# First attention: the values products put between the maxima and the scores of the next step, the maxima turned a step later, and all of the input biased ahead of the routing

## The reference

```python
x = layernorm(x + attention0(x))   # 16 heads of 8, causal, score - (i - j)
x = layernorm(x + mixture(x))      # 8 experts, each token goes to one: argmax(x @ centroids.T)
x = layernorm(x + attention1(x))   # 16 heads of 64, a gated distance bias, causal
x = layernorm(x + ffn(x))          # gated, 512 wide
# attention0 ends in  out @ Wo.T + bo ; the mixture starts with a layer norm of each token
```

## Time and profile before

| | us |
|---|---|
| median of 3 runs | 2271.55 (2269.65 to 2274.39) |
| the profiled execution, its own time | 2270.39 |
| its span in the trace | 2268.6 |
| first attention | up to 554.1 |
| routing: barrier to the last scatter issued | 554.5 to 624.2 |
| PE busy, whole span | 91% |

### The profile page before, as it was taken

The page is one execution under the profiler, slowest core; times in us unless marked ns, Lnnn a source line. Parts: engine busy times, 40 slices in busy tenths (PEclk is TensorE's granted clock), DMA queues, the critical chain, the costliest instruction groups (busy, mean ns, idle before and its releaser), DMA issues.

```text
span 2268.6 us, 34364 instructions
## 1 busy us (share of the span) xinstructions
PE 2053.4 (91%) x11728; PEld 1167.7 (51%) x11728; DVE 1373.6 (61%) x3345; ACT 1157.6 (51%) x1859; POOL 843.4 (37%) x544
## 2 busy tenths in 40 slices
PE   5799999998487879886899999999999999999998
PEld 2333333334476445444566556655666556655644
DVE  4777777774732678875566666666667655333311
ACT  2366666667343667674455555555555543223232
POOL 5000000000601445432577777777777773000000
PEclk8899999999589899996899999999999999999999
DMA  5233333111365579977667766776677677543300
GB/s 178 96 128 129 127 114 127 57 51 59 103 184 146 171 221 323 282 221 203 148 160 178 180 162 157 179 180 164 154 180 179 167 208 186 136 98 84 89 5 10
DMA packets 263468, 335.88 MB, mean 148 GB/s; under 512 B 22828, under 2 KB 185948, under 8 KB 262888
## 3 DMA queue, kind: packets, MB, share of 16 engines
q1 hardware_dynamic: 247992, 305.82, 50.2%
q0 software_dynamic: 7664, 24.39, 3.0%
q10 hardware_dynamic: 7640, 3.48, 0.5%
HBM read 193.69 MB, written 122.62 MB: 139 GB/s over the span
## 4 chain that ended last, share of the span: by engine, by line
PE 42%; issue 6%; DVE 4%; DMA 1%; SPq 0%; ACT 0%; DVEq 0%; ACTq 0%
PE ps L1284 10%; PE ps L953 7%; PE ps L937 6%; PE ps L906 6%; PE ps L938 6%; PE ps L1235 3%; DVE a1mx L1009 2%; PE ps L940 1%; PE ps L1295 1%; PE ps L1272 1%; PE ps L1273 1%; DVE a1mx L1005 1%; DMA a1FQ<-s_q 1%; DVE a1mx L1002 0%; PE ps L909 0%
## 5 line engine op out<-in xcount | busy, mean ns | idle before, releaser
L1120 POOL TENSOR_TENSOR a1sum<-a1sum,a1prob 128x1024 f32<-128x1024 f32 (+3 forms) x256 | 463.8, 1812 | 84.0 <-ACT a1prob L1063 51.2
L1063 ACT ACTIVATE a1prob<-ps 128x512 f32<-128x512 f32 (+2 forms) x640 | 328.0, 553 | 245.8 <-PE ps L940 214.5
L476 DVE TENSOR_REDUCE a0grid<-ps 128x8 f32<-128x1024 f32 x288 | 346.9, 1221 | 116.5 <-PE ps L351 71.9
L1002 DVE CUSTOM_DVE_ANT_0 ps<-ps,c_mask_ij 128x128 f32<-128x128 f32 x496 | 264.4, 551 | 194.3 <-issue 190.0
L577 ACT ACTIVATE a0prob<-ps 128x1024 f32<-128x1024 f32 x288 | 292.6, 1025 | 171.6 <-PE ps L377 91.5
L937 PE MATMUL ps<-a1QA,a1KA 69*128 69x512 f32 (+3 forms) x768 | 285.6, 379 | 5.0 <-DMA a1QA<-a1neg 5.0
L953 PE MATMUL ps<-a1prob,a1V 128*64 128x512 f32 (+3 forms) x1536 | 273.8, 499 | 5.0 <-ACT a1prob L1063 5.0
L938 PE MATMUL ps<-a1QB,a1KB 128*128 128x512 f32 (+3 forms) x768 | 264.3, 352 | 0.0
L906 PE MATMUL ps<-a1KA,a1QA 68*128 68x128 f32 x744 | 225.0, 381 | 4.6 <-DMA a1KA<-s_g 3.8
L953 PEld LDWEIGHTS ps<-a1prob,a1V 128*64 128x64 f32 x1536 | 102.9, 138 | 173.3 <-issue 138.7
L1005 DVE TENSOR_REDUCE a1mx<-ps 128x1 f32<-128x320 f32 x248 | 146.0, 589 | 70.5 <-PE ps L906 67.6
(11 more groups left out here) (267 smaller groups left out, 3196.1 us busy)
## 6 DMA issues: line engine op xcount, KB each, us to landing
a1FQ<-s_q SPq DMA_DIRECT2D x128, 256.0 KB, 7.9
a1KB<-s_k SPq DMA_DIRECT2D x128, 256.0 KB, 8.5
s_xs<-c_zero POOLq DMA_DIRECT2D x19, 1024.0 KB, 8.9
s_q<-mqkT SPq DMA_DIRECT2D x32, 512.0 KB, 3.4
s_v<-mv SPq DMA_DIRECT2D x32, 512.0 KB, 5.8
s_k<-a1KH SPq DMA_DIRECT2D x32, 512.0 KB, 5.0
s_k<-a1KL SPq DMA_DIRECT2D x32, 512.0 KB, 6.0
a1KA<-s_k SPq DMA_DIRECT2D x64, 256.0 KB
```

The source lines that it names most:

```text
L476: dve.tensor_reduce(grid[g % 2][:, :, a:b + 1:b - a], banks(("max", k)), axis=AX.X, op=ALU.max).then_inc(s1_free, 1)
L1002: dve.tensor_tensor_reduce(bank[:, 0:w], bank[:, 0:w], const["mask_ij"][:, BANK - w:BANK], 1.0, LOWEST, ALU.add, ALU.max, mx[:, x % 2, h, ...
L1063: act.activation(weights_of(g, u)[:, group[0]:group[-1] + 1, off:BANK], both(e, u, group), ACT.Exp).then_inc(weighed, 1)
L1120: pool.tensor_tensor(t[:, :, off:BANK], t[:, :, off:BANK], weights_of(g, u)[:, :, off:BANK], ALU.add).then_inc(summed, 1)
```

## The change

In the loop of PE, the values of the step before are issued between the maxima and the scores of a step, and the maxima are turned when k % NU is 2 instead of 1. In the routing, `x1` moves to memory that the first attention leaves free. SP loads the whole input into it ahead of the barrier, in two transfers of 1 MB, after the five small weights, and POOL biases all 8 chunks there ahead of the barrier, in place. `join` reads its chunk from `x1`, and `norm` writes it back there. Between the scatters POOL has nothing else to do, and SP has no loads to wait for.

```diff
-                if k % NU == 1 and NU < k <= TOTAL + 1:
+                if k % NU == 2 and NU < k <= TOTAL + 2:
                     turn_maxima(k // NU - 1)
+                if k > LEAD:
+                    g, u = divmod(k - 1 - LEAD, NU)
+                    if u in after:
+                        ...  # values(g - 1, r) and values(g, r), as below
                 if k < LEAD:
                     continue
                 g, u = divmod(k - LEAD, NU)
                 if g < GROUPS:
                     scores(k - LEAD)
-                if u in after:
-                    for r in after[u][0] if g > 0 else ():
-                        values(g - 1, r)
-                    for r in after[u][1] if g < GROUPS else ():
-                        values(g, r)
...
         def sync_ahead():
+            for d, s in first:
+                nc.sync.dma_start(d, s).then_inc(w_first, 16)
             load(0)
-            load(1)
-            for d, s in first: ...
+            load(1)          # load(half): 16 of the 32 tiles of x into x1
         def sync_first():
             ...
-            load(2)
             for d, s in rest:
                 nc.sync.dma_start(d, s).then_inc(w_rest, 16)
-            for c in range(3, steps):
-                load(c)
...
-                dve.tensor_tensor(r1[c % 2][:, :, :], tiles(ps[:, c % 2, :]), x[c % 2][:, :, :], ALU.add)
+                dve.tensor_tensor(r1[c % 2][:, :, :], tiles(ps[:, c % 2, :]), x1[:, c * TILES:(c + 1) * TILES, :], ALU.add)
...
         def gpsimd_ahead():
+            pool.wait_ge(w_first, 16 * len(first))
+            for c in range(steps):
+                pool.wait_ge(x_in[c // (steps // 2)], 16)
+                to = x1[:, c * TILES:(c + 1) * TILES, :]
+                pool.tensor_tensor(to, to, bo[:, :].unsqueeze(1).to_broadcast([P, TILES, P]), ALU.add).then_inc(biased, 1)
         def gpsimd_first():
             # only the 4 scatters of each chunk, no bias between them
```

More of the change, by code:

```diff
@@ L439, in tensor_program @@
                     drained(NPROD - 1)
-                if k % NU == 1 and NU < k <= TOTAL + 1:
+                if k % NU == 2 and NU < k <= TOTAL + 2:
                     turn_maxima(k // NU - 1)
+                if k > LEAD:
+                    g, u = divmod(k - 1 - LEAD, NU)
+                    if u in after:
+                        for r in after[u][0] if g > 0 else ():
+                            values(g - 1, r)
+                        for r in after[u][1] if g < GROUPS else ():
+                            values(g, r)
                 if k < LEAD:
@@ L1475, in middle @@
         jpos = own("jpos", [P, steps, TILES])
-        x1 = own("x1", [P, NTILE, P])
         stats, mv = own("st", [P, TILES, 6]), own("mv", [P, TILES, 2])
@@ L1504, in middle @@
         own("gap", [P, max(0, const["a0_end"] - nc.sbuf_base) // 4 + 8])
-        tri_f, x = own("trif", [P, P]), [own(f"xin{r}", [P, TILES, P]) for r in range(2)]
+        tri_f, x1 = own("trif", [P, P]), own("x1", [P, NTILE, P])
         wo, bo, cent = own("wo", [P, P]), own("bo", [P, P]), own("cent", [P, experts])
@@ L1529, in middle, with load @@
         PER = 6
[L1533 to L1537, removed]
+        def load(half):
+            t = slice(half * NTILE // 2, (half + 1) * NTILE // 2)
+            nc.sync.dma_start(x1[:, t, :], ins["x"][t.start * P:t.stop * P, :].rearrange("(t p) d -> p t d", p=P)).then_inc(x_in[half], 16)
         def sync_ahead():
+            for d, s in first:
+                nc.sync.dma_start(d, s).then_inc(w_first, 16)
             load(0)
             load(1)
-            for d, s in first:
-                nc.sync.dma_start(d, s).then_inc(w_first, 16)
         def sync_first():
@@ L1654, in join @@
                     dve.wait_ge(x1_full, c - 1)
-                dve.tensor_tensor(r1[c % 2][:, :, :], tiles(ps[:, c % 2, :]), x[c % 2][:, :, :], ALU.add).then_inc(joined, 1)
+                dve.tensor_tensor(r1[c % 2][:, :, :], tiles(ps[:, c % 2, :]), x1[:, c * TILES:(c + 1) * TILES, :], ALU.add).then_inc(joined, 1)
                 dve.wait_ge(joined, c + 1)
@@ L1824, in scalar_first, with gpsimd_ahead @@
             act.activation(om1[:, :], om1[:, :], ACT.Ln, bias=1.0).then_inc(rooted_u, 1)
-        def bias(c):
+        def gpsimd_ahead():
             pool = nc.gpsimd
[L1830 to L1837, removed]
+            pool.wait_ge(w_first, 16 * len(first))
[3 more added lines that the diff above has]
+                pool.tensor_tensor(to, to, bo[:, :].unsqueeze(1).to_broadcast([P, TILES, P]), ALU.add).then_inc(biased, 1)
         def gpsimd_first():
@@ L1842, in gpsimd_first @@
             pool.wait_ge(const["zeroed"], 16 * const["n_zeroed"])
[L1843 to L1852, removed]
+            for c in range(steps):
+                pool.wait_ge(dest_full, c + 1)
+                pool.wait_ge(xn_full, (c + 1) * TILES)
+                for t in range(TILES):
+                    pool.indirect_dma_start(scr["xs"][:, :], bass.IndirectOffsetOnAxis(dest[:, c * TILES + t:c * TILES + t + 1], 0),
+                                            xn[c % NS][:, t, :], None).then_inc(sent[c % NS], 16)
         loaded = [sem(f"loaded{r}") for r in range(NX)]
```

## The result

The changed kernel takes 2256.8 us, median of 17 executions, against 2271.9 for the kernel before on the same chips: ratio 0.9925 (0.9907 to 0.9943). The forecast was 2251.5, in a range of 2240 to 2264. Its profiled execution took 2246.6 us of its own, at the fast end of its runs, so the medians and the places in the trace are compared before the span is.

What follows compares the result with a forecast made beforehand. In attention no engine is full, PE and DVE wait in turns; POOL's scatters set the routing's end. Profiled 2270.4 us less 11.7 (attention) and 8.3 (routing) is 2250.4; with the median 1.2 above, forecast 2251.5, range 2240 to 2264.

Steps and rivals of the forecast that it cites:

- 28.97 a group: First attention: PE's timetable of 18 steps puts a group at 28.97 us against 29.76, 0.8 us less.
- 11.7 us: First attention's saving: 0.8 us a group over 14.7 groups; bounds 0 and 73.
- "nothing" was forecast: First attention's first 24 steps (no values) and last 24 (no maxima): old sequence on PE, so no gain taken.
- 1.62 us from S to the M it holds: Attention timetable: scores S(k-2) to maxima products M(k), through ScalarE's exponential; 1.02 plus an assumed 0.06 release, 1.62 us.
- The two steps taken as the example: Attention, M (maxima products) of U = 2 to M of U = 4: old 3.25 us, new 3.14.
- Rival B: Attention's waits only move from S to M, ACT's release costing more than 0.06; routing as summed: 2263 us; chance 0.14.
- C: Rival, attention: slots come free sooner, half of the 5.0 us of waits goes, 37 us, so 2226; chance 0.07.
- Rival E: Attention: loop of exponential, M, values, S binds; group takes 30.6 us, total 2276; chance 0.04.
- Nothing waits, cost 0: Attention, turning the maxima later: transposition done some 1 us before U = 2's reduction ends, so cost 0.
- then DVE takes 5.39 a chunk: Routing without biases between scatters: DVE 5.39 us a chunk, POOL 5.06; last scatter ends at 615.9, saving 8.3 us.
- lower bound of 4.7: Routing's saving of 8.3 us: at least 4.7, if only the first wait goes; upper bound 10.5.
- Rival D: Routing: packed scatters held up by DVE's copies and normalization, 0.26 us each for 32, returning 8.3 us: 2260; chance 0.04.

Runs made afterwards that it cites:

- e2: Kernel before with both attention edits (values moved, maxima turned a step later) and the routing of before; 2259.2 us, ratio 0.9956.
- e1: The whole change run once more, no edit against the kernel after; 2258.6 us, ratio 0.9942 to the kernel before.
- e8: Kernel after with each exponential of two blocks issued as two instructions; one execution, negations 29.28 us apart.
- e9: Kernel before with each exponential of two blocks issued as two instructions; one execution, 2263.7 us, where the kernel before took 2263.8 on the same chip.
- e4: Kernel before with only the values moved in the attention, maxima turned where they were, routing of before; 2256.3 us, ratio 0.9938.
- e5: Kernel after with the maxima turned a step earlier, where the kernel before turned them; 2251.1 us, ratio 0.9918.
- e3: Routing alone: kernel after with PE's old order in the attention; 2263.7 us, ratio 0.9965 to the kernel before.
- e11: Kernel after with the 32 scatters issued from GpSimd as plain stores to fixed rows, not sorted by expert; one execution, 2248.4 us.
- e10: Kernel after with scatters replaced by SyncE's plain stores and GpSimd doing four adds of 128x512 a chunk instead; one execution, 2272.0 us.

## Why the prediction was right, and where it was not

**Attention: right, by its own steps.** Forecast 28.97 a group, measured 28.86; end at 542.4, measured 542.9; 11.7 us, measured 11.2 and in e2 11.8. Counted from M of U = 4 at 258.25, the next eighteen M stand within 0.23 us of the forecast's places. The nearness of the total is partly luck. The 0.9 us that a group gained would make 13.2 over 14.7 groups; the twelve intervals gave 10.8, the last negation to the end lost 0.4 where "nothing" was forecast, and the 0.8 ahead of the third negation is less than that place moves between executions (e1). The number that no row of before could show, 1.62 us from S to the M it holds, stands in the trace twice as 1.62. S waits for DVE 2.1 us a group (1.5 forecast, 5.6 before) and M for ACT 3.1 (2.5 forecast, 1.0 before), so one wait was swapped for a shorter one on another engine, as described. The two steps taken as the example gained nothing, however: 3.26 us from M of U = 2 to M of U = 4, where 3.14 was forecast and 3.25 was the old time. The gain is made in the other sixteen. Rival B, that the release by ACT costs more, and C, that half of the waits go, are out: both need another interval than 28.9. Rival E is not what happens, but e8 and e9 show what it was made of: the exponential now stands on the path, and 3.2 us more of it cost 0.42.

**One step of that part was wrong: a cost put at nothing.** "Nothing waits, cost 0" was said of the later turn. Moved back, the group is 0.22 us shorter (e4, e5), and attention 2.6 us from the third negation on (399.0 against 401.6). The trace after shows why it can't be free: the transposition stands between M of U = 2 and the values (255.42 to 255.64), 0.22 us in the chain values, S, exponential, M of U = 4, which is one that binds.

**Routing: the mechanism was right, its size half.** Join 3 without a wait, L1694 at 0.16 in all chunks, the small operation at 0.18 instead of 1.01, no bias between scatters, scatters 1.27 us apart, no wait for the input: all as forecast. First scatter 563.29, which is 20.4 us after attention's end where 20.0 was forecast. Then it parts: from the first scatter to the end of the last it is 45.5 us (563.29 to 608.78) where 41.8 was forecast (574.1 to 615.9). Beyond the usual 0.30 between scatters, POOL was to wait 1.3 us in all for destinations, and it waited 4.7, nearly all at two places (2.93 at 576.22, 2.08 at 588.48), each time behind a halt of DVE (2.47 at join 5, 1.52 at 587.62). These 3.7 us more and the 0.4 of the start are the shortfall: the last scatter ends 65.9 us after the attention, not 62. The step that failed is "then DVE takes 5.39 a chunk", which lets every release come at once; some came 1.5 to 4.6 us late. The two long halts, at chunk 7, cost nothing here: GpSimd was behind by then, and its last four scatters followed without a wait. So 4.2 us came of 8.3, 3.3 in e1 and 3.8 in e3, below the forecast's own lower bound of 4.7. The kernel before has none of these halts and e9 has none, so they came with the change, and with either half of it: 5.8 and 5.3 us at locate 6 in e2 and e4, 9 to 16 us in all with the new routing. In the four kernels with the old routing the stretch is 68.7 to 70.6 us; in the seven with the new one and scatters it is 64.6 to 69.2, mean 66.3 against 69.7. Where the halts fall decides what such a kernel loses. With plain stores (e11), without halts and with 0.54 us a store instead of 0.97, the experts begin 12 us earlier after the barrier.

Rival D, scatters starved behind DVE's copies, priced a shortfall of this kind from the wrong side. But for one of 1.18, scatters behind the first stay near 0.97 us and 1.27 apart; it is DVE that waits. The rule of the Trainium skill behind D ("SBUF — State Buffer", "SBUF: two separate sides") tells of GpSimd's descriptors waiting for DVE; no row here shows that.

**The rest of the difference.** Forecast 2251.5, median 2256.8: 4.1 of the 5.3 us are the routing's. That the profiled execution came out at 2246.6 is no merit of the change. From the last scatter's end to the program's end, the same code took 1635 to 1649 us over the eleven traces with such scatters (after 1636.0, e1 1648.1, before 1644.4, e9 1637.3), in no order of old and new; over all fourteen the granted clock lay between 0.946 and 0.956. An effect of the change there is not seen, and one of under 5 us can't be excluded.

**Open.** What delays the releases isn't settled, nor what has to come on top of the scatters: before and e9 have them and no late release. The ends of PE's products are modelled, so they may themselves have been late, but DVE's own step at 586.10 was released 1.5 us late as well. The traces with late releases also lack 1 to 7 of the 40 records of PE's, those without lack none; that the recording of the trace has a part in it is not excluded. Choose 7 restarts within 0.1 us of a scatter's start in six of the seven traces with the new routing and scatters (598.63 and 598.67 in that of after), but not in e8's. The wait of 2 to 4 us at join 3 in before, e2, e4 and e9 is another thing: it ends 0.1 us after the bias of chunk 3, as the forecast has it.

## What to carry to other kernels

When an operation is moved past another in a loop that two engines take turns in, write out the loop's timetable with every instruction on it, small ones too: it gave the group to 0.4% here, and the transposition that it put at 0.18 us on the path was the one I then called free. Look-up scatters can cost the engines beside them too, not only the one that issues them: here half of what the routing was to give was lost in waits for late releases. Where a wait has no cause in the timeline, compare the end of the work with the time at which its semaphore moved, before saying which engine stands still. And where runs of one kernel spread by 15 us, take a change's worth from distances between places in the trace (negations, barriers), and check that the medians agree.

## What the runs showed of the hardware that was not expected

Beside GpSimd's look-up scatters, semaphore releases can come 1 to 6 us behind the ends of the PE products that give them, several in a row and then together; DVE then waits, 10 us in a stage of 65. None of the 40 is late beside plain stores of the same size from GpSimd (0.54 us each instead of 0.97) or from SyncE, and none in the kernel before with the same scatters. Destinations in order don't help. A GpSimd add of 128x512 can make small DVE operations with two on-chip inputs three to almost six times as long (0.19 to 0.58 and 0.78 us, 0.17 to 0.94 for L1698 of e10), and left the one with an input in the accumulation memory alone (0.19). Cutting an exponential of 1,024 columns in two costs ScalarE 0.18 us each, and the kernel 0 to 0.42 us a group of 18.
